# The residual of the attention is added outside TensorE, and the first norm's statistics come from ScalarE

## The reference

```
x = x + gnn(layernorm(x), adj)
x = x + ffn(layernorm(x))

gnn(x):  q, k, v = x @ Wq.T + bq, x @ Wk.T + bk, x @ Wv.T + bv       # 4 heads of 32
         scores = clip(q . k / sqrt(32), -10, 10), set to -10 where adj is 0
         attn   = softmax over each chunk of 128 keys alone (8 chunks)
         ctx    = sum over the chunks of attn @ v
         out    = ctx @ Wo.T + bo + x                                # the residual of the change
         return (out - mean(out)) * rsqrt(var(out) + eps) * gamma + beta
ffn(x):  the two best of 8 experts by x @ Wg + bg; sum of gelu(x @ W1 + b1) @ W2 + b2 over the two
```

## Time and profile before

| | before |
|---|---|
| device time, median of 3 runs | 728.84 us (728.39 to 732.42) |
| the profiled execution | 730.68 us, its span 728.9 us |
| TensorE busy | 691.0 us, 95% |
| VectorE busy | 605.4 us, 83% |
| GpSimd busy | 563.2 us, 77% |
| ScalarE busy | 503.5 us, 69% |

### The profile page before, as it was taken

How to read it: one execution, slowest core, us unless ns; L and a number is a source line. 1 busy time by engine, 2 the same in 40 slices (tenths; PEclk the granted TensorE clock), 3 DMA queues, 4 the chain that set the end, 5 groups by cost and what they waited for, 6 DMA issues and landing times.

```text
span 728.9 us, 17234 instructions
## 1 busy us (share of the span) xinstructions
PE 691.0 (95%) x5510; PEld 362.8 (50%) x5510; DVE 605.4 (83%) x1387; ACT 503.5 (69%) x1017; POOL 563.2 (77%) x616
## 2 busy tenths in 40 slices
PE   8988999999999999999999999989889999999994
PEld 6322233333333323333333333323378899999994
DVE  4789989999999999999999999999897656555552
ACT  4755577787777778677787777666677567667662
POOL 8659586988889898988989889898776776555553
PEclk9998999999999999999999999999999999999997
DMA  7541010010111101111010010014241254333400
GB/s 262 190 130 30 1 30 16 15 45 30 37 38 30 45 16 45 38 38 44 16 45 23 24 45 15 30 37 125 60 129 57 96 154 127 99 95 95 111 28 2
DMA packets 47960, 45.44 MB, mean 62 GB/s; under 512 B 6981, under 2 KB 42576, under 8 KB 47872
## 3 DMA queue, kind: packets, MB, share of 16 engines
q1 hardware_dynamic: 41888, 31.60, 15.1%
q0 software_dynamic: 5984, 12.74, 5.0%
HBM read 27.73 MB, written 18.34 MB: 63 GB/s over the span
## 4 chain that ended last, share of the span: by engine, by line
PE 69%; DVE 15%; issue 7%; ACT 5%; DMA 1%; POOL 1%; DVEq 1%; SPq 1%; POOLq 0%; ACTq 0%
PE scores_ps L454 15%; PE ctx_ps L466 11%; PE scores_ps L630 10%; PE z_ps L473 9%; DVE e L1006 9%; PE ctx_ps L656 5%; PE z_ps L656 5%; ACT x_rows L783 3%; PE job_ps L502 2%; PE job_ps L529 2%; PE job_ps L493 2%; PE job_ps L565 2%; PE job_ps L514 1%; PE job_ps L564 1%; PE scores_ps L616 1%
## 5 line engine op out<-in xcount | busy, mean ns | idle before, releaser
L778 ACT ACTIVATE e<-e 128x2048 f32<-128x2048 f32 x128 | 245.1, 1915 | 145.3 <-DVE e L1006 145.3
L1006 DVE SCALAR_TENSOR_TENSOR e<-scores_ps,bound_mem 128x2048 f32<-128x2048 f32 x128 | 293.2, 2291 | 27.7 <-PE scores_ps L454 22.1
L882 ACT ACTIVATE e<-scores_ps,bound_mem 128x128 f32<-128x128 f32 x364 | 104.4, 374 | 51.0 <-PE scores_ps L630 50.4
L1510 POOL DMA_INDIRECT out<-e,near x91 | 91.1, 1002 | 61.6 <-DVE e L1230 48.7
L473 PE MATMUL z_ps<-e,one_column 128*32 128x512 f32 x1024 | 134.7, 597 | 0.0
L1491 POOL TENSOR_TENSOR ctx_part<-ctx_part,z_inv 128x1024 f32<-128x1024 f32 x60 | 115.7, 1929 | 23.2 <-DVE z_inv L1022 23.2
L1503 POOL TENSOR_TENSOR ctx_sum<-ctx_sum,ctx_part 128x512 f32<-128x512 f32 x90 | 115.4, 1282 | 8.4 <-POOL ctx_sum L1503 0.9
L630 PE MATMUL scores_ps<-e,bound_mem 128*128 128x128 f32 x728 | 97.0, 276 | 4.0 <-ACT e L853 2.1
L1014 DVE STREAM_TRANSPOSE ctx_part<-ctx_ps 128x512 f32<-128x512 f32 x128 | 90.3, 706 | 1.6 <-PE ctx_ps L466 1.6
L630 PEld LDWEIGHTS scores_ps<-e,bound_mem 128*128 128x128 f32 x728 | 88.5, 192 | 5.6 <-ACT e L853 3.9
L1465 POOL DMA_INDIRECT sorted_rows<-x_rows,slot x64 | 63.6, 994 | 19.3 <-issue 16.4
(11 more groups left out here) (188 smaller groups left out, 1011.6 us busy)
## 6 DMA issues: line engine op xcount, KB each, us to landing
near<-sorted_rows SPq DMA_DIRECT2D x91, 130.0 KB, 2.1
near<-in_x SPq DMA_DIRECT2D x16, 256.0 KB, 2.8
bound_mem<-in_adjT SPq DMA_DIRECT2D x4, 1024.0 KB, 9.0
x_post<-in_x SPq DMA_DIRECT2D x16, 256.0 KB, 2.7
sorted_rows<-pad_row SPq DMA_DIRECT2D x1, 3640.0 KB, 15.1
out<-e,near POOLq DMA_INDIRECT x91, 2.3
sorted_rows<-x_rows,slot POOLq DMA_INDIRECT x64, 2.6
bound_mem<-in_w SPq DMA_DIRECT2D x1, 1024.0 KB, 5.4
```

The lines of the kernel that those rows point to most:

```text
L778: nc.scalar.activation(every, every, ACT.Exp, scale=SCORE_SCALE).then_inc(exp_done, 1)
L882: nc.scalar.activation(e_flat[:, h_at:h_at + P], scores_ps[:, i % 2, k * P:(k + 1) * P], ACT.Gelu, bias=part_flat[:, bias_at:bias_at + 1]) ...
L1006: dve.scalar_tensor_tensor(out=e[:, s % E_RING], in0=scores_ps[:], scalar=-CLIP, in1=to, op0=ALU.max, op1=ALU.min).then_inc(clipped, 1)
L1510: nc.gpsimd.indirect_dma_start(out=out_rows, out_offset=bass.IndirectOffsetOnAxis(ap=near_u[:, id_at:id_at + 1], axis=0), in_=e_flat[:, at ...
```

## The change

- TensorE's `project` no longer transposes: it only multiplies. The residual (normalised x plus the output's bias) is kept untransposed: GpSimd writes it as `xn_bo` (`add_bias`, one add of 128x512 per block, after `scale` 4; for the first three blocks before the loop, behind the masks). VectorE adds it to the projection into `residual`, in SBUF (`add_residual`, j3). ScalarE's `square_proj` and `normalise_proj`, at their old places in its queue, read `residual`. The bias is laid out as a row (`bo_all`), and ScalarE's second copy `xnT_bo` is gone.
- From block 3 on, norm 1's statistics are taken by ScalarE: `sum_x` (j4) and `square_x` (j5), four activations with an accumulator each, in place of VectorE's. GpSimd's root then computes the variance first.
- `find_places` moves from j3 to j4. `normalise_x(v)` also waits for the bias add of block v-2, whose buffer it overwrites. `rank` and `mark_pair` wait for the residual in place of the scaled rows.
- The rings `XT_RING` and `O_RING` have one buffer less each.

```diff
-XT_RING, XN_RING, W_RING, H_RING, O_RING = 16, 3, 3, 3, 14
+XT_RING, XN_RING, W_RING, H_RING, O_RING = 15, 3, 3, 3, 13
...
             def keys(v):
-                if v == 0:
-                    pe.wait_ge(xnT_ready, 1)
-                else:
-                    pe.wait_ge(xnT_bo_ready, v + 1)
+                pe.wait_ge(xnT_ready, v + 1)
...
             def rank(v):
                 pe.wait_ge(one_hot_ready, v + 1)
-                need(pe, n2_ready, done(v + 1))
+                need(pe, residual_ready, done(v + 1))
...
-                    pe.transpose(job_ps[1][:, cols], xnT_bo[:, v % 4, cols], ident[:])
-                    ins = pe.matmul(job_ps[1][:, cols], ctxT[:, cols], wo_centred[:], start=False, stop=True,
-                                    skip_group_check=True)
+                    ins = pe.matmul(job_ps[1][:, cols], ctxT[:, cols], wo_centred[:], start=True, stop=True)
...
             def normalise_x(v):
                 need(act, xnT_filled, v - 1)
+                need(act, xn_bo_ready, v - 1)
                 normalise(ln["1"], v, xn[:, v % 2], x_in[:, v % 2])
+            def sum_x(v):
...
+                for t in range(TILES):
+                    ins = nc.scalar.activation(unused[:, t, :], x_in[:, v % 2, t, :], ACT.Copy, scale=-1.0 / D,
+                                               accum_out=l["minus"][:, t, :])
+            def square_x(v):
...
+                for t in range(TILES):
+                    ins = nc.scalar.activation(unused[:, t, :], x_in[:, v % 2, t, :], ACT.Square, bias=l["minus"][:, t, :],
+                                               accum_out=l["mv"][:, t, 1:2])
             def square_proj(v):
                 need(act, x2_ready, v)
                 need(act, var2_ready, v)
-                act.wait_ge(proj_filled, v + 1)
+                act.wait_ge(residual_ready, v + 1)
...
-                nc.scalar.activation(xnT_bo[:, v % 4, :], turned_ps(v)[:], ACT.Identity, bias=bo_all[:, 0:1])\
-                    .then_inc(xnT_bo_ready, 1)
...
+                    if j == 4 and is_block(u + 3):
+                        sum_x(u + 3)
+                    if j == 5 and is_block(u + 3):
+                        square_x(u + 3)
...
+            def add_residual(v):
+                dve.wait_ge(proj_filled, v + 1)
+                dve.wait_ge(xn_bo_ready, v + 1)
+                need(dve, n2_ready, v)
+                dve.tensor_tensor(residual[:], job_ps[1][:].rearrange("p (t d) -> p t d", d=D), xn_bo[:, v % 4], ALU.add)\
+                    .then_inc(residual_ready, 1)
...
-                    if j == 1 and u > 0 and is_block(u + 3):
-                        begin_statistics_x(u + 3, range(0, 1))
...
+                    if j == 3 and is_block(u - 2):
+                        add_residual(u - 2)
...
-                        if j == 3:
+                        if j == 4:
                             find_places(u - 3)
-                        if j == 4:
                             mark_pair(u - 3)
-                    if j == 4 and is_block(u + 3):
-                        begin_statistics_x(u + 3, range(1 if u else 0, TILES))
...
-                    if j == 6 and is_block(u + 3):
-                        end_statistics(ln["1"], u + 3)
...
                 if k == 1:
+                    add_residual(14)
                     scale_last(4)
...
+                if k == 8:
+                    add_residual(15)
...
-                nc.gpsimd.tensor_tensor(both["minus"][:], both["mv"][:, :, 0:1], minus_one[:], ALU.mult)\
+                nc.gpsimd.tensor_scalar(ln["1"]["var"][:], ln["1"]["mv"][:, :, 1:2], 1.0 / D, LN_EPS, ALU.mult, ALU.add)
+                nc.gpsimd.tensor_tensor(ln["3"]["minus"][:], ln["3"]["mv"][:, :, 0:1], minus_one[:, 0:TILES], ALU.mult)\
                     .then_inc(both_minus, 1)
+                pool.wait_ge(both_minus, roots["both"])
                 nc.gpsimd.tensor_tensor(both["rstd"][:], both["var"][:], minus_half[:], ALU.pow).then_inc(both_rstd, 1)
-                pool.wait_ge(both_minus, roots["both"])
...
+            def add_bias(v):
+                need(pool, residual_ready, v - 3)
+                pool.wait_ge(ln["1"]["s_out"], v + 1)
+                if v == 0:
+                    pool.wait_ge(bias_ready, 1)
+                nc.gpsimd.tensor_tensor(xn_bo[:, v % 4], xn[:, v % 2], bo_all[:].to_broadcast([P, TILES, D]), ALU.add)\
+                    .then_inc(xn_bo_ready, 1)
...
             for c in range(HALF0_D + 2, CHUNKS):
                 prepare_bound(0, c)
+            for v in range(3):
+                add_bias(v)
             for u in range(BLOCKS):
...
                 if is_block(u - 1):
                     scale(u - 1, 4)
+                if u > 0 and is_block(u + 2):
+                    add_bias(u + 2)
```

More of the change, by code:

```diff
@@ L145, in graph_transformer_layer @@
         bo_sb = sb("bo_sb", [P, 1])
-        bo_all = sb("bo_all", [P, 1])
+        bo_all = sb("bo_all", [P, 1, D])
         bv_all = sb("bv_all", [P, 1])
@@ L162, in graph_transformer_layer @@
         xnT = near[:, 5 * SEQ:6 * SEQ].rearrange("p (a n) -> p a n", a=2)
-        xnT_bo = sb("xnT_bo", [P, 4, BLOCK])
+        xn_bo = sb("xn_bo", [P, 4, TILES, D])
+        residual = sb("residual", [P, TILES, D])
         q_last, k_last = sb("q_last", [P, BLOCK]), sb("k_last", [P, SEQ])
@@ L216, in graph_transformer_layer @@
                 for name, size in (("mv", 3), ("minus", 1), ("var", 1), ("rstd", 1), ("shift", 1))}
+        unused = sb("unused", [P, TILES, D])
         mean_square, var2, rstd2 = (sb(name, [P, TILES, 1]) for name in ("mean_square", "var2", "rstd2"))
@@ L310, in graph_transformer_layer @@
         ctxT_ready = sem("ctxT_ready")
-        xnT_filled, xnT_ready, xnT_bo_ready = sem("xnT_filled"), sem("xnT_ready"), sem("xnT_bo_ready")
+        xnT_filled, xnT_ready, xn_bo_ready = sem("xnT_filled"), sem("xnT_ready"), sem("xn_bo_ready")
+        residual_ready = sem("residual_ready")
         k_filled, k_ready = sem("k_filled"), sem("k_ready")
@@ L676, in _ @@
             pe.wait_ge(bv_ready, 1)
-            pe.matmul(z_ps[:, D:D + 1], wo_centred[:], bv_all[:], start=True, stop=False)
-            pe.matmul(z_ps[:, D:D + 1], centre[:], bo_sb[:], start=False, stop=True).then_inc(bias_filled, 1)
+            pe.matmul(z_ps[:, D:2 * D], bv_all[:].to_broadcast([P, P]), wo_centred[:], start=True, stop=False)
+            pe.matmul(z_ps[:, D:2 * D], bo_sb[:].to_broadcast([P, P]), centre[:], start=False, stop=True)\
+                .then_inc(bias_filled, 1)
             keep_busy(2)
@@ L788, in normalise_x @@
                 need(act, xnT_filled, v - 1)
+                need(act, xn_bo_ready, v - 1)
                 normalise(ln["1"], v, xn[:, v % 2], x_in[:, v % 2])
-            proj_rows = job_ps[1][:].rearrange("p (t d) -> p t d", d=D)
+            def sum_x(v):
+                l = ln["1"]
+                act.wait_ge(l["s_shift"], v)
+                act.wait_ge(l["s_var"], v)
+                act.wait_ge(x_loaded[v % 2], 16 * (v // 2 + 1))
+                for t in range(TILES):
+                    ins = nc.scalar.activation(unused[:, t, :], x_in[:, v % 2, t, :], ACT.Copy, scale=-1.0 / D,
+                                               accum_out=l["minus"][:, t, :])
+                ins.then_inc(l["s_mv"], 1)
+            def square_x(v):
+                l = ln["1"]
+                act.wait_ge(l["s_mv"], v + 1)
+                for t in range(TILES):
+                    ins = nc.scalar.activation(unused[:, t, :], x_in[:, v % 2, t, :], ACT.Square, bias=l["minus"][:, t, :],
+                                               accum_out=l["mv"][:, t, 1:2])
+                ins.then_inc(l["s_var"], 1)
             def square_proj(v):
@@ L795, in square_proj @@
                 need(act, var2_ready, v)
-                act.wait_ge(proj_filled, v + 1)
+                act.wait_ge(residual_ready, v + 1)
                 for t in range(TILES):
-                    ins = nc.scalar.activation(n2[:, t, :], proj_rows[:, t, :], ACT.Square, scale=1.0 / float(np.sqrt(D)),
+                    ins = nc.scalar.activation(n2[:, t, :], residual[:, t, :], ACT.Square, scale=1.0 / float(np.sqrt(D)),
                                                accum_out=mean_square[:, t, :])
@@ L804, in normalise_proj @@
                 for t in range(TILES):
-                    ins = nc.scalar.activation(n2[:, t, :], proj_rows[:, t, :], ACT.Copy, scale=rstd2[:, t, :])
+                    ins = nc.scalar.activation(n2[:, t, :], residual[:, t, :], ACT.Copy, scale=rstd2[:, t, :])
                 ins.then_inc(n2_ready, 1)
@@ L895, in _ @@
             drain_q(0)
-            add_output_bias(0)
+            act.wait_ge(bias_filled, 1)
+            nc.scalar.activation(bo_all[:, 0, :], z_ps[:, D:2 * D], ACT.Copy).then_inc(bias_ready, 1)
             normalise_x(1)
@@ L1444, in root @@
                 roots[l["name"]] += 1
```

(9 more changed lines are left out.)

13 lines of the change are left out of this document (removed).

## The result

The changed kernel takes 768.4 us (median of 4 runs, 765.3 to 772.33) against 729.5 for the kernel before on the same chip: ratio 1.0528, 95% interval 1.0503 to 1.0554, 38.9 us slower. The forecast was 759, in a range of 745 to 777. The profiled execution has a span of 770.6 us, 41.7 more than before. One of the ten executions of a later run, the one with VectorE's add one step earlier, took 1333.45 us; its ratio leaves that one out, and its median without it is 734.52.

The account below looks back on a forecast made before the run. GpSimd's loop, released late by the squares, was to set the block: start 4.7, blocks 2 to 12 23.1, block 13 1.4, blocks 14 and 15 0.5, end 0.8, together +30.5 us, giving 759 against the median; range 745 to 777.

Parts of the forecast that it names:

- GpSimd's loop (A): Blocks 2 to 12: GpSimd, released late by the squares, sets a period of 33.5 us; +2.1 each, 23.1; chance 0.63.
- ScalarE's delay: Blocks 2 to 13: squares wait for VectorE's add, so the keys start at t = 16.0; 1.4 us lost per block.
- The gain in j1 and j2: Half projections in j1 and j2 lose two TensorE transposes each, VectorE loses statistics: 0.3 us gained for the two.
- rival C: TensorE's idle time before the keys lowers its clock each block: at most 1.7 us, +18 on A, 777; chance 0.12.
- Block 13, and 14 and 15: Block 13 loses only ScalarE's 1.4 us; blocks 14 and 15, without a keys product, +0.5 us for both.
- Start: Blocks 0 and 1: normalising of block 2 waits 5.3 us for block 0's bias add; in all +4.7 us (3.5 to 6.5).
- the low clock after TensorE's 6.02 us of idle time: Block 0, after about 6 us of idle TensorE: a lowered clock costs 1.5 us.
- The mask's wait: First clip of block 1: its 1.39 us wait for GpSimd's mask goes, credited as -1.4 us.
- the slow stretch behind it: Block 1: the low-clock stretch after the mask's wait goes, worth 0.7 us (0 to 1.7).
- End: First experts' tiles: two VectorE adds of 0.69 come in, eight TensorE transposes go; +0.8 us (-2.6 to +1.4).
- the smaller rings: Expert part: rings with one buffer less cost nothing while TensorE is busy; otherwise the tile pace would grow.
- The new add beside GpSimd: VectorE's residual add keeps its 0.69 us beside GpSimd; if locked out, 0.7 us more per block, 8 in all.

Follow-up runs that it names:

- the last run: Residual add in j2 and block 0's bias add ahead of the last two masks, on the changed kernel, with norm 1's statistics back on VectorE: 730.53 us, ratio 0.9983.
- the fillers: Changed kernel plus five TensorE multiplications by zero columns in j4 of blocks 2 to 13, during the wait for the keys' input: 762.69 us, ratio 1.0447.
- the run with two moves: Changed kernel with VectorE's residual add in j2 and GpSimd's bias add of block 0 ahead of the last two masks: 725.93 us, ratio 0.9933.

## Why the prediction was right, and where it was short

**GpSimd's loop (A): right.** The squares started at t = 12.57 (12.55 predicted), GpSimd needed 19.59 us from the squares' release to the end of its last sum (19.8), that sum ended at 33.53 (33.5 to 33.6). With the clock's part taken out, every block lasts 33.44 (33.5). VectorE's add is 0.66 (0.69 taken), the bias add 1.28 (1.29). But in the changed kernel as it stands the loop seldom shows: in block 7 the sum of t = 33.53 is there before the next start, which the clock has put to 34.42, and VectorE waits ahead of L1055 only in blocks 3, 5, 9 and 11, 0.48 to 0.52 us each. And of the 2.05 us by which a block without the clock's part is longer than before, ScalarE's delay alone gives 1.58.

**ScalarE's delay: right, 0.2 low.** The keys start at t = 16.18, not 16.0: the squares hold the exponential of j3 back until 13.76, not 13.55 (the prediction's own rows, 12.55 + 0.91 + 0.22, add up to 13.68). The block without the loop is 32.97, not 32.8.

**The gain in j1 and j2: right.** j1 to j2 fell from 4.63 to 4.46, j2 to j3 from 3.74 to 3.62: 0.29 (0.3). The transposes are 0.2 of it: with the statistics back on VectorE, in the last run, the two are 4.57 and 3.60.

**The clock: the term that failed.** I had TensorE's idle time before the keys as rival C, in all blocks at up to 1.7 us, with 0.12, and nothing for it in A. It happened on top of A, in eight of blocks 2 to 13: the clock falls to its lower level (1.2 of 2.4 GHz; the mean is 0.69 over 277.00 to 281.23) after the wait and j4 lasts 6.4 to 7.05 us instead of 5.85. I had argued from the wait of 1.53 us that left the clock alone and the one of 2.13 that did not the earlier trace rows; the waits here, 1.79 and 1.88, lie between and do both. Taking it out moved the stretch from block 2 to the start of 14 from 409.0 to 400.5 us in the profiled executions. These 8.5 us are most of the 11 by which the sum was short there. By the ratios the fillers save 5.9 us (0.0081 of 730), of the 9.4 by which 759 was short: executions differ in how much the clock falls. The four of the changed kernel have a mean clock of 0.969, 0.971, 0.978 and 0.981 and spans of 770.6, 768.8, 764.6 and 763.6 us, the profiled one being the longest. So 768.4 lies within A's own range, 754 to 769, by luck in part: that range was made for a slower add or root, and what filled it is a part of C. The Trainium skill ("TensorE: Matmul & The Clock Gate", section "What's actually happening") has a low clock as the default that activity lifts; the fillers agree, as with them the clock stays at 1.00 over the blocks in which it fell.

**Block 13, and 14 and 15: short by 1.6 and 1.9.** In 13 the clock is 0.97 of it (34.42, with fillers 33.45); the rest is GpSimd's loop, which I had ended at block 12 while its late sum still held up the start of 13 (by 0.52 in the run with fillers). In 14 and 15, which have no keys, I took GpSimd out of the sum; but its late x2 rows hold up VectorE's statistics in j5, by 1.07 us in block 14 (timeline of VectorE, changed kernel):

```profile
521.44 0.88 DVE L981 BATCH_NORM_STATS2 ln_stats<-x_rows 128x6 f32<-128x128 f32 x4 [1.07 <-POOL x_rows L1494]
```

In the run with GpSimd's order changed block 14 lasts 30.51 us, against 31.62 in the changed kernel and 30.38 before.

**Start: right in mechanism, 1.3 low.** The normalising started 5.3 us later, counted from the first clip (17.26 after it, 11.99 before). The mask's wait went as credited (the last step of block 0 is 1.37 shorter), the slow stretch behind it nearly so (block 1 is 0.56 shorter, 0.7 taken). The mis-sized term is the low clock after TensorE's 6.02 us of idle time: steps j3 to j5 of block 0 are 8.1 us longer, so 2.8 beside the wait, where I took 1.5 from a shorter idle stretch. The scores there take 2.09 us, and the 6 us behind have a clock of 0.61.

**End: +1.44 against +0.8.** 0.9 of it is there at the first tile finished (17.33 us after the last clip, 16.44 before), 1.4 by the twentieth and the same at the last. So it arises among the first tiles, where the two adds stand; a loss from the smaller rings would grow with the tiles. Which instruction it is, no run separates, nor is it a fixed price: in the run with fillers, which stand in blocks 2 to 13 alone, the part takes 211.22 us, 0.24 more than before.

**The new add beside GpSimd.** In the changed kernel this could not be judged, as GpSimd idles during the add of every block but the last. In the run with two moves the add takes 0.67 us beside a GpSimd add, not the 1.36 of the earlier trace rows. The Trainium skill ("SBUF — State Buffer", section "Who interferes with whom") spares a VectorE add with one PSUM input and one in SBUF; that run agrees.

## What to carry to other kernels

Moving work off the busiest engine pays only if its result is ready when the next in-order queue reaches the instruction that reads it: here an add of 0.66 us, one step too late, cost 1.6 us per block through ScalarE's queue, then 0.5 through GpSimd's, then the clock. Before a new dependence is written, list what stands behind the waiting instruction in its queue, and try the producer one step earlier; here that and one bias add ahead of two masks turned +5.3% into -0.7%, of which, by the last run, the residual's move alone gives 0.2 and the statistics on ScalarE the rest. A reordering that fills a wait is worth nothing, and may cost, once the wait itself is gone: test moves together, not only one by one.

## What the runs showed of the hardware that was not expected

Idle stretches of TensorE equal in length had opposite outcomes. In the changed kernel the scores took 1.14 us after 1.79 before the keys of block 8, and 2.09 after 1.88 before those of block 7. In the kernel with GpSimd's order changed 1.88 us stand before the keys of both block 5 and block 7, and the scores differ in the same way (TensorE in block 5, then in block 7):

```profile
209.40 1.18 PE L493 MATMUL job_ps<-near,w_proj 128*128 128x512 f32 x2 [1.88 <-ACT near L826]
210.51 2.09 PE L457 MATMUL scores_ps<-near 32*128 32x512 f32 x8
...
276.79 1.13 PE L493 MATMUL job_ps<-near,w_proj 128*128 128x512 f32 x2 [1.88 <-ACT near L826]
277.85 1.14 PE L457 MATMUL scores_ps<-near,k_last 32*128 32x512 f32 x8
```

The length of the wait alone does not tell whether the clock falls; what else decides it stays open. 1.25 us of matmuls with zeros, cutting the idle rest to 0.8 us, left no long block among 3 to 13.
